# VectorE seeds the y banks with D times the input, and the row stack is loaded in 32-row pieces

## What is computed

```python
xr, gate = split(x @ W_in.T)                      # 2 x 1024 wide
xc = silu(causal_conv4(xr + t_emb) + b_conv)
xn = layernorm(xc) * ln_g + ln_b                  # "the input" of the recurrence
Bm, Cm, dt = split(xn @ W_xproj.T)                # 16 wide each
dt = tanh(dt @ W_dt.T + b_dt) * 0.01
Ad = 1 + dt * -tanh(A_log);  Bd = Bm * min(norm(xn), 1)
h_t = clip(h_{t-1} * Ad_t + Bd_t * xn_t, -10, 10)  # state 16 x 1024, over 2048 tokens
y_t = C_t . h_t + D * xn_t
out = x + (y * silu(gate)) @ W_out.T
```

## Time and profile before

| | us |
|---|---|
| median of 3 runs | 2229.75 |
| the profiled execution, its own time | 2229.9 |
| its span | 2228.1 |
| TensorE (PE) busy | 2016.9 (91%) |
| VectorE (DVE) busy | 1762.9 (79%) |
| ScalarE (ACT) busy | 1434.6 (64%) |
| GpSimd (POOL) busy | 1818.6 (82%) |
| chain that ended last: PE / SP queue / ACT / DMA | 35% / 23% / 13% / 12% |

### The profile page before, as it was taken

One profiled execution on the slowest core, in us unless ns is written; L12 is line 12 of the kernel. 1 busy time (PEld: TensorE's weight loads), 2 busy tenths in 40 slices (PEclk: granted clock), 3 DMA queues, 4 the chain that ended last, 5 costly groups with the idle time before them and its releaser, 6 DMA issues.

```text
span 2228.1 us, 47105 instructions
## 1 busy us (share of the span) xinstructions
PE 2016.9 (91%) x16976; PEld 1458.5 (65%) x16976; DVE 1762.9 (79%) x2080; ACT 1434.6 (64%) x3462; POOL 1818.6 (82%) x1444
## 2 busy tenths in 40 slices
PE   5599999999999999999999999999999999999888
PEld 4366666666666666666666666666666666666654
DVE  2388888788888788888788888788888878888886
ACT  4576666676666676666666666666666667666642
POOL 1288888888888888888888898888888888888876
PEclk8599999999999999999999999999999999999999
DMA  4111111121111121111111111111111112111110
GB/s 164 51 56 42 53 40 51 57 61 46 49 41 51 56 60 46 50 41 51 56 60 47 51 45 46 55 60 56 44 53 40 53 59 61 40 55 39 46 53 15
DMA packets 77777, 117.05 MB, mean 53 GB/s; under 512 B 17941, under 2 KB 46997, under 8 KB 72933
## 3 DMA queue, kind: packets, MB, share of 16 engines
q1 hardware_dynamic: 77544, 114.04, 16.5%
HBM read 59.47 MB, written 9.18 MB: 31 GB/s over the span
## 4 chain that ended last, share of the span: by engine, by line
PE 35%; SPq 23%; ACT 13%; DMA 12%; issue 8%; DVE 6%; POOL 2%; DVEq 0%; POOLq 0%; ACTq 0%
DMA xs<-xl 11%; SPq L340 9%; SPq L341 9%; PE ps_job L490 7%; PE ps_y L575 6%; SPq L345 5%; PE ps_job L449 5%; PE ps_fill L548 4%; ACT low L769 4%; ACT tap L728 4%; PE ps_fill L539 3%; DVE ks L975 3%; PE ps_job L456 2%; PE ps_job L462 2%; POOL prod L1073 2%
## 5 line engine op out<-in xcount | busy, mean ns | idle before, releaser
L1073 POOL TENSOR_TENSOR prod<-ks,crep 128x512 f32<-128x512 f32 x1024 | 1305.1, 1288 | 292.3 <-PE ps_y L575 265.6
L975 DVE TENSOR_TENSOR_SCAN ks<-low,ps_fill 128x512 f32<-128x512 f32 x1024 | 1227.7, 1210 | 284.1 <-PE ps_fill L548 274.6
L769 ACT COPY low<-ps_fill 128x512 f32<-128x512 f32 x1024 | 594.0, 580 | 594.4 <-PE ps_fill L539 588.3
L575 PE MATMUL ps_y<-c_sb,prod 128*128 128x128 f32 x4096 | 621.3, 274 | 0.7 <-POOL prod L1073 0.6
L575 PEld LDWEIGHTS ps_y<-c_sb,prod 128*128 128x128 f32 x4096 | 465.9, 141 | 113.1 <-issue 50.9
L548 PE MATMUL ps_fill<-spans,pick 128*128 128x512 f16 x1024 | 393.2, 384 | 121.1 <-ACT low L769 117.1
L539 PEld LDWEIGHTS ps_fill<-ts,xs 128*128 128x128 f16 x4096 | 314.4, 98 | 150.2 <-issue 4.9
L539 PE MATMUL ps_fill<-ts,xs 128*128 128x128 f16 x4096 | 397.0, 219 | 2.9 <-DMA xs<-h 2.9
L548 PEld LDWEIGHTS ps_fill<-spans,pick 128*128 128x128 f16 x1024 | 99.3, 97 | 236.4 <-ACT low L769 193.7
L728 ACT ACTIVATE tap<-xr,cols_sb 128x128 f32<-128x128 f32 x768 | 251.7, 392 | 0.1
L444 PE MATMUL ps_job<-x,w_in 128*128 128x128 f16 x3072 | 215.2, 221 | 15.3 <-POOL x L1043 7.8
(11 more groups left out here) (126 smaller groups left out, 2373.1 us busy)
## 6 DMA issues: line engine op xcount, KB each, us to landing
crep<-c_dram SPq DMA_DIRECT2D x32, 1024.0 KB, 4.7
xs<-xh SPq DMA_DIRECT2D x256, 62.0 KB
xs<-xl SPq DMA_DIRECT2D x224, 64.0 KB
xf<-in_xT SPq DMA_DIRECT2D x32, 256.0 KB, 2.8
res<-in_x SPq DMA_DIRECT2D x32, 256.0 KB, 2.7
out_dram<-res SPq DMA_DIRECT2D x32, 256.0 KB, 2.1
ts<-tth SPq DMA_DIRECT2D x128, 32.0 KB
ts<-tth SPq DMA_DIRECT2D x128, 31.0 KB
```

The costliest lines, as they stand in the source:

```text
L575: last = mm(ps_y[:, u // 4, cut], prod[:, s % HOLD, e, :], ident, start=False, stop=(u % 4 == 3 and q == 3 and e == QN - 1), is_transpose= ...
L769: copy(low[:, s % RING], ps_fill[:, s % RING]).then_inc(sem["low_copied"], 1)
L975: nc.vector.tensor_tensor_scan(ks[:, u % 2, QN * q:QN * (q + 1)].rearrange("d n t -> d (n t)"), low[:, s % RING], ps_fill[:, s % RING], 0. ...
L1073: tt(prod[:, i % HOLD], ks[:, u % 2, part], crep[:, p, part], ALU.mult).then_inc(sem["weighed"], 1)
```

## The change

The y banks are no longer opened by a matmul. VectorE writes D times xn into each bank as soon as its last block has been read (`skip` on VectorE, at points 43 and 9), and every matmul into the bank adds to it. Two matmuls at the start, with operands that are zero, open the banks once. GpSimd's product, the buffer `xd`, the identity product and the semaphores xd_done and xd_used are gone. The copies of `xh` are moved whole, 32 rows a piece. The rows of ones are written over their first rows by two DMAs in each period, which wait until the row stack has landed; the fill waits for them (ones_in).

```diff
-                for r in (0, 32):
-                    loads.append((xs[r:r + 1, p], A["ones16"].rearrange("o (j d) -> o j d", j=NSUB)))
...
-                        sp.dma_start(xs[1:SUB, pn, jj], xh[a + 1:a + SUB]).then_inc(xstack, 16)
-                        sp.dma_start(xs[SUB + 1:2 * SUB, pn, jj], xh[a + 1:a + SUB]).then_inc(xstack, 16)
+                        sp.dma_start(xs[0:SUB, pn, jj], xh[a:a + SUB]).then_inc(xstack, 16)
+                        sp.dma_start(xs[SUB:2 * SUB, pn, jj], xh[a:a + SUB]).then_inc(xstack, 16)
...
                     sp.dma_start(crep[:, pn]..., c_dram...).then_inc(sem["c_in"], 16)
+                    sp.wait_ge(xstack, N_XSTACK * pair(k, p, 1))
+                    for r in (0, SUB):
+                        sp.dma_start(xs[r:r + 1, pn], A["ones16"].rearrange("o (j d) -> o j d", j=NSUB)
+                                     ).then_inc(sem[f"ones_in{pn}"], 16)
...
+            for i in range(2):
+                last = mm(ps_y[:, i], pick[:], spans[:, 0, 0:BANK], start=True, stop=True)
+            last.then_inc(sem["y_opened"], 1)
...
-                    pe.wait_ge(sem[f"xstack_in{p}"], N_XSTACK * pair(k, p, 0))
+                    pe.wait_ge(sem[f"ones_in{p}"], N_ONES * pair(k, p, 0))
...
             def base(k, p, i):
-                since(pe, "y_gated", 2 * (k - 1) + i + 1)
-                mm(ps_y[:, i], mT[:, p], xn[:, p, half], start=True, stop=False)
+                pe.wait_ge(sem["skip_set"], 2 * k + i + 1)
+                mm(ps_y[:, i], mT[:, p], xn[:, p, half], start=False, stop=False, skip_group_check=True)
...
-            def skip(k, p, i):
-                if i == 0:
-                    pe.wait_ge(sem["xd_done"], k + 1)
-                last = mm(ps_y[:, i], ident, xd[:, i * BANK:(i + 1) * BANK], start=False, stop=False)
-                if i == 1:
-                    last.then_inc(sem["xd_used"], 1)
...
+            def skip(k, p, i):                                  # on VectorE
+                half = slice(i * BANK, (i + 1) * BANK)
+                dve.wait_ge(sem["xn_done"], k + 1)
+                since(dve, "y_gated", 2 * (k - 1) + i + 1)
+                if k == 0:
+                    dve.wait_ge(sem["y_opened"], 1)
+                tt(ps_y[:, i], xn[:, p, half], row_d[:, half], ALU.mult).then_inc(sem["skip_set"], 1)
...
+                        if point == 43 and exists(k, 1):
+                            skip(k + 1, 1 - p, 0)
+                        if point == 9 and exists(k, 0):
+                            skip(k, p, 1)
...
-                    if s == 9 and exists(k, 0):
-                        if exists(k, 1):
-                            pool.wait_ge(sem["xa"], k + 2)
-                        pool.wait_ge(sem["xn_done"], k + 1)
-                        tt(xd[:], xn[:, p], row_d[:], ALU.mult).then_inc(sem["xd_done"], 1)
```

More of the change, by code:

```diff
@@ L71 @@
 res_in out_done0 out_done1 const_in fixed_in
-xstack_in0 xstack_in1 stack_in0 stack_in1 bound_out bound_in0 bound_in1
+xstack_in0 xstack_in1 ones_in0 ones_in1 stack_in0 stack_in1 bound_out bound_in0 bound_in1
 gw_ready wdt_ready wdt_set sums_ready sums_taken halo_set prep prepared act_prep
@@ L79 @@
 halo_saved conv_taken stats aggr rstd moments z1 zb ad scan_p recip weighted bound32 bound16 bound_all p_kept
-norm_in xa xg xn_done xh_done xl_done yT_high squares root nrm nb16 tt_done xd_done xd_used kend_done c_out c_in
+norm_in xa xg xn_done xh_done xl_done yT_high squares root nrm nb16 tt_done skip_set y_opened kend_done c_out c_in
 y_gated h1_done carry16
@@ L179, in build @@
         ones = gate[:, 0:P]
-        xd = xc
         res = sb("res", [P, DM])
@@ L255, in build @@
         N_CONST = 16 * 5
-        N_FIXED = 16 * 9
+        N_FIXED = 16 * 5
+        N_ONES = 16 * 2
         N_XSTACK = 16 * 3 * NSUB
@@ L411, in _ @@
             pe.wait_ge(sem["gw_ready"], 2)
+            pe.wait_ge(sem["spans_clear"], 3)
             for i, src in enumerate((gw, bw)):
@@ L569, in flip @@
                     base(k, p, s // (4 * NQ))
-                if s in (3 * NQ, 4 * NQ):
-                    skip(k, p, s // NQ - 3)
                 pe.wait_ge(sem["weighed"], TILES * k + s + 1)
@@ L575, in flip @@
                     last = mm(ps_y[:, u // 4, cut], prod[:, s % HOLD, e, :], ident, start=False,
-                              stop=(u % 4 == 3 and q == 3 and e == QN - 1), is_transpose=True)
+                              stop=(u % 4 == 3 and q == 3 and e == QN - 1), is_transpose=True,
+                              skip_group_check=True)
                 last.then_inc(sem["flipped"], 1)
@@ L733, in side @@
                     since(act, "xa", k + 2)
-                    since(act, "xd_used", k + 1)
                     act_fn(xc[:, i * BANK:(i + 1) * BANK], bank("conv", i), ACT.Silu).then_inc(sem["conv_taken"], 1)
```

## The result

The changed kernel takes 2165.53 us, the median of 4 runs (2164.48 to 2165.86), against 2228.45 (4 runs). The ratio is 0.9717, with a 95% interval of 0.9703 to 0.9731: 63 us less, where 88 were forecast. The page's busy row answers to the earlier trace rows. TensorE (PE) lost 67 us of work and GpSimd 49, and VectorE has 12 more. Neither of the last two is the size of what was moved. GpSimd lost a product of 75.4 us, but two of its rows grew by 27.7 us together beside VectorE's new products (L1036, 552 to 973 ns in the mean, and L1049, 2128 to 2571).

What follows compares the result with a forecast made beforehand. PE was taken as at its bound for 93% of a 66.47 us period, idling 4.63 us, partly through ScalarE's wait for the row stack. 2229.9 − 68.7 − 27.5 − 0.9 + 9.3 = 2142.1 us; range 2112 to 2180.

Steps and rivals of the forecast that it cites:

- The wait for the stack goes: ScalarE's wait at L745 for the row stack's last DMA vanishes with 32-row pieces: 68.7 us, 10.1 in the start-up.
- The steady waits count whole: ScalarE's 1.89 us stack wait in each of the other 31 periods counts fully as time won.
- The first identity product is paid out of the wait: PE's first L561 product per period lies under ScalarE's 1.82 us stack wait, so its 0.86 us is not counted again.
- The second identity product: PE's second L561 product per period stands where PE waits for nobody, so removing it wins 32 × 0.86 = 27.5 us.
- GpSimd's product, nothing on the path: Removing GpSimd's L1030, 2.36 us × 32, wins nothing on the path; bounds nothing to 75.4 us.
- rows of ones, nothing: Two DMA issues per period need 1.3 us of SP's 5.8 us wait for ttl, so cost nothing.
- VectorE's products: Two new products a period, 0.7 us each alone, make scans late; 0.3 a period, 9.3 us; bounds −0.6 to 4.3.
- Tiles between scan and refill: Banks refill four tiles after their scan and tiles flip four after filling, so most lateness never reaches PE.
- The signs of being wrong: Pieces still issuing in 2.3 us; L548 newly waiting for ScalarE; VectorE's scans releasing fills and GpSimd's products.
- B: Rival: VectorE's products reach the path, 1.8 us a period instead of 0.3, time 2188.6; chance 0.14.
- C: Rival: ScalarE becomes the bound; at worst the upper identity product frees nothing, time 2169.6; chance 0.14.
- E: Rival: PE's other waits shrink too, 0.6 us a period, nothing lost to VectorE, time 2114; chance 0.15.

Runs made afterwards that it cites:

- e4: The changed kernel with VectorE's clip of the state moved from point 28 to 36, behind both carries: 2142.15 us, ratio 0.9610.
- e2: The changed kernel with the old 31-row pieces back and ones loaded once, so the y half alone: 2205.68 us, ratio 0.9891.
- e1: The kernel before with only the row stack's half applied (32-row pieces, ones in each period), identity products kept: 2181.84 us, ratio 0.9788.
- e3: The changed kernel with VectorE's two products a period left out, so D times the input is missing from y: 2155.47 us, ratio 0.9666.
- e9: e1 with VectorE's clip of the state moved from point 28 to 36: 2178.98 us, ratio 0.9774.
- e7: The changed kernel with the clip at point 36 and VectorE's upper product at point 24 instead of 9: 2133.80 us, ratio 0.9568.

## Why the prediction was right or wrong

The forecast of 2142.1 us was 23 too low. The direction, the range and most steps held.

- *The wait for the stack goes.* Right, and for the reason given: issue near 0.6 us, stack in early. Start-up, put at 10.1 us: the start of the second period came 11.3 us earlier (L663 at 105.35 against 116.68).
- *The steady waits count whole, 58.6 us.* This is the step that failed. ScalarE's 1.82 us and the lower identity product under it were indeed won together, 1.79 us by slot 17. But 0.83 came back one slot later, so that 0.96 a period was kept, about 30 us of the 58.6. I had read VectorE's L931 only as evidence for a price, and had not asked what stood behind it once ScalarE was no longer late: clip, scan and L955 stand in one queue, and the scan ends at 1069.75, when ScalarE has only just been let go (1069.24). Let ScalarE go earlier, and that queue is what is late. 0.83 × 31 is 26 us, and e4 got 23 of them back.
- *The first identity product is paid out of the wait.* Right for the kernel before (e2: nothing won by it). In the changed kernel it is only partly paid: e1 against e3, with the same slot 18 (27.65) with and without it, shows that the carry's wait for VectorE took its place, until the clip moves (e9 against e7, 27.48 against 26.83, 0.65 us for the product).
- *The second identity product, 27.5 us.* Right: 0.86 us a period, between slots 18 and 21.
- *GpSimd's product, nothing on the path; rows of ones, nothing.* Not contradicted. GpSimd's busy time fell by 49 us, not by the 75 that were expected. SP still waits for ttl behind the ones, as this row of its waits shows, against the earlier trace rows. GpSimd's product was not tried alone.

```profile
SPq L381 <- POOL ttl L1059: 188.7, 32, 6.4
```

- *VectorE's products, 0.3 us a period (9.3 us).* The size was right, 0.33, and 10 us by e3, though 0.3 was a choice between bounds and not worked out, so that is luck in part. The route was wrong: not late scans but a late GpSimd, two steps further on. The scan behind the upper product came 1.0 us late (1.2 was given), and itself did no harm. The lower product, for which the contended case was priced at 3.1 us, took 0.70 at 1047.66. GpSimd's L1049 came in behind it and was the one held, 2.58 us instead of 2.12, as the timelines of VectorE and GpSimd in the changed kernel show:

```profile
1046.89 0.67 DVE L959 TENSOR_TENSOR gate<-ps_y,gate 128x512 f32<-128x512 f32 x1
1047.66 0.70 DVE L968 TENSOR_TENSOR ps_y<-xn,row_d 128x512 f32<-128x512 f32 x1
1048.28 2.32 DVE L980 TENSOR_TENSOR_SCAN ks<-low,ps_fill 128x512 f32<-128x512 f32 x2
```

```profile
1047.77 2.58 POOL L1049 TENSOR_TENSOR h<-h 16x1024 f16<-16x1024 f32 x1
```

- *Tiles between scan and refill.* The forecast said that most lateness of a scan never reaches PE, since a bank is filled again four tiles after its scan and flipped four after its fill. By the code these are three slots (the wait for `scanned` in `fill`) and six. No fill waits for a scan in the changed kernel, so the conclusion stood, with less room at the refill than was thought.
- *The signs of being wrong.* None of the three that were named came: the pieces issue in 0.6 us, no widening waits for ScalarE where the old gap was, and no fill waits for a scan (GpSimd's products wait for scans 32.7 us in all, 24.0 before). What came, a wait of a carry product of PE for VectorE, was not among them.
- Of the rivals, none was the cause. B put a cost of this size on VectorE's new products; it was VectorE, but with its old work. C put it on ScalarE, which is dense in that stretch, yet e4 sped it up without touching ScalarE. Its time, 2169.6, is 4 us from the measured one by chance: in C the upper product frees nothing, and here it freed its 0.86 us whole. E expected more than the forecast, and less came.

Terms as measured: 11.3 for the start-up, 1.56 × 31 = 48.4 for the periods, and some 4 at the end, which were not traced, make the 64 us between the two spans.

## What to carry to other kernels

When a wait goes, list for each engine what it will have finished at the new, earlier time, its own queue included: a stall of one engine hides the long instruction of another, and that one is the next bound. Price an instruction beside the engine that it shares a resource with, at the place where it will stand, and look at who comes after the other engine, not only after this one. A DMA's row count is worth a look at the DMA share: 0.07 with full rows of 2 KB is about one engine of sixteen at work.

## What the runs showed that I had not expected

The same instruction, the 16x1024 clip, took 2.65 us at point 28 and 0.655 at point 36, and the half us more went to GpSimd's next instruction. A 128x512 product took 1.55 us or 0.70 by where it stood, and in the first case it held a 0.55 us instruction of GpSimd to 1.00. And a loss can vanish: the 0.33 us that VectorE's product costs in e2 is absorbed by ScalarE's wait, so the same edit has another price in each kernel.
